# Norm products of local queries and keys: from VectorE to GpSimd, with a re-sorted order of units

## Chip, cores and metric

The kernel runs on one core of one Trainium2 chip. The metric is the device time of one execution in microseconds; the median of three runs is compared. A profiled execution gives the trace.

## What is computed

The input is `x` (4 batches, 512 tokens, 128 features) with a small context of 77 tokens per batch. Each batch goes through three parts:

- **A:** a cross attention of 16 heads to the context, then a layer norm;
- **two local layers**, each a local attention of 8 heads of 64 with windows of 64 tokens, and a gated feed-forward part;
- **C:** a second cross attention with a bias on its scores, then a feed-forward part with activations rounded to 8-bit integers.

The change lies in the local attention. Its queries and keys are normalised per head and turned by a rotary table:

```
q, k = l2norm(q) * q_scale, l2norm(k) * k_scale      # per head of 64
q = q * cos * scale + rotate_half(q) * sin * scale
k = k * cos / scale + rotate_half(k) * sin / scale
sim = einsum(q * 8, k) in windows of 64 and the 64 tokens before
out = softmax(masked sim) @ v;  x = x + out @ wo
```

The inverse norm is a factor per token and head, so the kernel turns first and multiplies by it last.

## The kernel before

Tokens lie on the 128 partitions; a batch is 4 tiles of 128 tokens. All work is cut into units (some instructions of one engine), in streams: X and V (cross attention: scores, values), Z (feed-forward of C, and the norm that ends A), P (projection, rotary and norm of local queries and keys), T (local scores), U (local output), F (local feed-forward). P, T, U and F each have 8 items, one for each batch and layer, in the order of `BLOCKS`. The text numbers them 0 to 7. Each engine plays its units in a fixed order, written in the table `ORDER` ("P3 U1" is three P units, then one U unit). An engine's instructions run strictly in that order, and every one waits by semaphores for what it needs. So a unit that waits holds up all units behind it on its engine.

One item of P goes like this. TensorE turns the input (L761) and projects it in 8 products `QK` (L768), a tile's queries and keys apart. ScalarE squares each bank (L957). VectorE multiplies the bank by cosine into `rot_a` (L1273) and by sine into `rot_b` (L1274), and sums the squares of each tile (L1277). GpSimd adds `rot_b` to `rot_a` (L589, one instruction of 128x1024 for each tile). When all four tiles are summed, VectorE works out 64 inverse norms for each token by Newton steps (L1025 to L1031, into `inv_norm`), and then multiplies each tile of `rot_a` by them in place (L1286, 128x1024, four instructions for each item, each in a unit of its own). Each signals `qk_ready`, on which TensorE waits before it transposes that tile (L780, called QKT here), the first step of T. The next item's cosine products into the same tile of `rot_a` wait for that transposition.

Others that matter: L1258 on VectorE copies half of the next item's projection input out of PSUM (`hT_l`), before which TensorE can't begin that item's L768. L596 on GpSimd multiplies the local probabilities by the inverse row sums that VectorE makes in L1302, and TensorE transposes them in L812. L1294 is VectorE's maximum of local scores, L1322 the gate of F, L1221 the hidden layer of C, L1332 the sum that ends a batch's local layers. L605, L610 and L557 are small GpSimd instructions of F and of the norms.

Of the kernel before, what the change touches and what calls it, by code (L numbers as in the profile page):

```python
# [154 lines left out]
def bank_order():  # L155
# [9 lines left out]
    for group in cross_groups():  # L165
# [11 lines left out]
        "Z2 U32 Z6",  # L177
    "gpsimd":
# [3 lines left out]
    "tensor":  # L182
# [14 lines left out]
    "scalar":  # L197
# [11 lines left out]
    "vector":  # L209
# [11 lines left out]
}  # L221


# [1165 lines left out]
```

## Time and profile before

| | |
|---|---|
| median of 3 runs | 790.55 us (790.01 to 792.83) |
| the profiled execution | 790.43 us |
| its span, first to last instruction | 788.5 us |
| TensorE busy | 618.3 us, 78% |
| VectorE busy | 579.0 us, 73% |
| ScalarE busy | 434.2 us, 55% |
| GpSimd busy | 198.7 us, 25% |

The busy shares are means over stages: a start in which batches' A parts run, a long middle in which the eight local items run, and an end with the C parts. The profiled execution lies 0.12 us under the median of the runs.

### The profile page before, as it was taken

The page shows a single profiled execution, that of the slowest core. Times are in us where ns is not written, and L with a number is a line of the kernel's source. Part 1 is how long each engine was busy: PE and PEld are TensorE (multiplying, and loading weights), DVE is VectorE, ACT ScalarE, POOL GpSimd, SP SyncE. Part 2 cuts the span into 40 slices and gives each one's busy share as a digit, 9 for nine tenths or more (in the row PEclk, how much of TensorE's full clock was granted, in tenths as well). Part 3 has the DMA queues.
Part 4 walks back from the last instruction along what each step waited for, and adds up shares of the span by engine and source line. Part 5 has one row for each costly group of instructions (what it writes and reads, how often), then busy time and mean ns, then how long its engine had stood idle before and what let it go on. Part 6 is the DMA issues. An engine that isn't in the chain of part 4 may idle for free.

```text
span 788.5 us, 15899 instructions
## 1 busy us (share of the span) xinstructions
PE 618.3 (78%) x6108; PEld 413.3 (52%) x6108; DVE 579.0 (73%) x1341; ACT 434.2 (55%) x1076; POOL 198.7 (25%) x133
## 2 busy tenths in 40 slices
PE   5777659879997876877886999678879988887622
PEld 3554434556656653645554565554466675555411
DVE  5659796786877466667658777897577758989965
ACT  2324316754767573586576478456765774632722
POOL 2001241332252144134343122321632121111010
PEclk9789978999999999999999999879989997885865
DMA  7380002001000200010200110002002000000000
GB/s 214 106 168 1 1 0 48 2 2 27 22 2 2 47 2 1 21 28 1 47 2 1 26 23 2 1 1 48 1 2 61 2 1 1 2 14 1 2 13 14
DMA packets 27975, 18.96 MB, mean 24 GB/s; under 512 B 14879, under 2 KB 23677, under 8 KB 27901
## 3 DMA queue, kind: packets, MB, share of 16 engines
q1 hardware_dynamic: 27180, 17.82, 9.5%
q8 instruction: 49, 0.80, 0.4%
q10 hardware_dynamic: 720, 0.13, 0.1%
q14 instruction: 26, 0.21, 0.1%
HBM read 9.56 MB, written 1.05 MB: 13 GB/s over the span
## 4 chain that ended last, share of the span: by engine, by line
PE 43%; DVE 28%; ACT 11%; issue 10%; SPq 4%; POOL 2%; DMA 1%; DVEq 0%; POOLq 0%; ACTq 0%
PE ps L768 6%; PE ps L692 5%; PE ps L856 4%; SPq L529 3%; ACT probs_l L974 3%; PE ps L656 3%; PE ps L793 3%; PE ps L833 3%; PE ps L805 3%; PE ps L812 2%; PE ps L780 2%; DVE rot_b L1274 2%; PE ps L863 2%; PE ps L680 2%; DVE probs L1145 2%
## 5 line engine op out<-in xcount | busy, mean ns | idle before, releaser
L596 POOL TENSOR_TENSOR probs_l<-probs_l,row_sum_l 128x1024 f32<-128x1024 f32 x32 | 63.4, 1981 | 223.5 <-DVE row_sum_l L1302 223.5
L974 ACT ACTIVATE probs_l<-ps,neg_max_l 128x128 f32<-128x128 f32 x256 | 90.6, 379 | 16.2 <-DVE neg_max_l L1294 16.0
L589 POOL TENSOR_TENSOR rot_a<-rot_a,rot_b 128x1024 f32<-128x1024 f32 x32 | 75.1, 2355 | 59.0 <-DVE rot_b L1274 59.0
L768 PE MATMUL ps<-wqkv,hT_l 128*128 128x512 f32 x128 | 72.1, 646 | 19.9 <-DVE rot_b L1274 16.2
L1273 DVE TENSOR_TENSOR rot_a<-ps,rot 128x512 f32<-128x512 f32 x64 | 43.9, 687 | 52.1 <-ACT squares L957 42.9
L920 ACT ACTIVATE probsT<-ps 128x512 f32<-128x512 f32 (+1 forms) x96 | 47.2, 527 | 45.2 <-PE ps L680 45.0
L656 PE MATMUL ps<-k_diag,hT 32*128 32x308 f32 x256 | 63.1, 533 | 10.1 <-DVE probs L1150 3.6
L856 PE MATMUL ps<-hT_f,w 128*128 128x512 f32 x96 | 52.9, 633 | 16.3 <-ACT gelu_g L1007 7.3
L957 ACT ACTIVATE squares<-ps 128x512 f32<-128x512 f32 x64 | 38.7, 605 | 48.1 <-PE ps L768 40.4
L680 PE MATMUL ps<-ident,probs 128*128 128x128 f32 x320 | 53.4, 301 | 6.0 <-ACT probs L909 1.9
L974 ACT ACTIVATION_READ_ACCUMULATOR probs_l<-ps,neg_max_l 128x1 f32 x256 | 56.0, 219 | 0.0
L909 ACT ACTIVATE probs<-probs 128x1232 f32<-128x1232 f32 x32 | 39.7, 1239 | 27.8 <-DVE probs L1150 16.8
L680 PEld LDWEIGHTS ps<-ident,probs 128*128 128x128 f32 x320 | 39.1, 153 | 26.9 <-issue 15.1
L823 PE MATMUL ps<-probsT_l,v_win 128*64 128x64 f32 x1024 | 38.5, 230 | 15.8 <-ACT probsT_l L988 15.6
L1294 DVE TENSOR_REDUCE neg_max_l<-ps 128x4 f32<-128x512 f32 x64 | 42.6, 683 | 10.8 <-PE ps L793 10.5
L988 ACT ACTIVATE probsT_l<-ps 128x512 f32<-128x512 f32 x64 | 35.3, 602 | 27.5 <-PE ps L812 27.3
L823 PEld LDWEIGHTS ps<-probsT_l,v_win 128*64 128x64 f32 x1024 | 34.3, 143 | 29.1 <-ACT probsT_l L988 19.6
L780 PE MATMUL ps<-ident,rot_a 128*128 128x128 f32 x256 | 39.1, 294 | 12.0 <-issue 5.6
L692 PE MATMUL ps<-probsT,v_flat 128*32 128x128 f32 x832 | 40.2, 307 | 10.4 <-ACT probsT L920 6.8
L692 PE MATMUL ps<-probsT,flat_ones 128*32 128x128 f32 x832 | 46.8, 300 | 0.0
L557 POOL TENSOR_TENSOR root_Z<-spread_Z,minus_half 128x4 f32<-128x4 f32 x16 | 16.2, 1012 | 120.6 <-DVE spread_Z L1041 73.8
L656 PEld LDWEIGHTS ps<-k_diag,hT 32*128 32x128 f32 x256 | 26.5, 206 | 36.1 <-issue 10.1
(165 smaller groups left out, 1374.4 us busy)
## 6 DMA issues: line engine op xcount, KB each, us to landing
v_win<-v_win SPq DMA_DIRECT2D x56, 128.0 KB, 2.3
score_bias<-fside_1x16xSxS SPq DMA_DIRECT2D x4, 616.0 KB, 8.7
wqkv<-L_ffn_wqkv SPq DMA_DIRECT2D x2, 768.0 KB
x_res<-x SPq DMA_DIRECT2D x4, 256.0 KB
out<-x_res SPq DMA_DIRECT2D x4, 256.0 KB, 2.3
w<-L_ffn_w SPq DMA_DIRECT2D x6, 128.0 KB
rot_a<-L_ffn_w SPq DMA_DIRECT2D x2, 256.0 KB, 4.2
probs_l<-c_rot SPq DMA_DIRECT2D x1, 512.0 KB
```

The costliest lines, as they stand in the source:

```text
L589: g.tensor_tensor(rot_a[:, t], rot_a[:, t], rot_b[:, t % 2], ALU.add).then_inc(rot_added.sem, 1)
L596: g.tensor_tensor(w, w, row_sum_l[:, t].unsqueeze(2).to_broadcast([P, LH, P]), ALU.mult).then_inc(probs_ready.sem, 1)
L656: mm(to[:, 0:GK].rearrange("p (h k) -> p h k", h=GH), hT[rows, tile(t)], k_diag[rows], start=True, stop=True, tile_position=(32 * grp, 0)) ...
L680: last = tr(to[:, tile(c - a)], probs[:, t % 2, tile(c)], ident)
L692: last = mm(to[32 * grp:32 * grp + 32, tile(part)], of[:, i], probsT[:, tile(c)], start=first, stop=final, tile_position=(0, 32 * grp), sk ...
L768: mm(to, hl[:, tile(t)], wqkv[:, l, k * INNER:(k + 1) * INNER], start=True, stop=True).then_inc(ps.fill(it, "QK", t, k), 1)
L780: last = tr(to[:, tile(c)], rot_a[:, t, tile(k * CH + c)], ident)
L823: last = mm(to[heads, c * P + j * WIN:c * P + (j + 1) * WIN], v_win[:, 2 * t + j, at:at + LD], probsT_l[:, half, c * P + j * WIN:c * P + ( ...
L856: mm(to, w1[:, l, (1 - k) * HC + c], hT_f, start=True, stop=True).then_inc(ps.fill(it, "F", c, k), 1)
L920: a(probsT[:, first * P:end * P], ps.bank(it, "PT", t, n)[:, 0:(end - first) * P], ACT.Copy).then_inc(ps.empty(it, "PT", t, n), 1)
L974: last = a(probs_l[:, t % 2, tile(hd)], ps.bank(it, "S", t, half)[:, tile(c)], ACT.Exp, bias=neg_max_l[:, t, hd:hd + 1], accum_out=row_sum ...
L1273: v.tensor_tensor(rot_a[:, t, cols].rearrange("p (h d) -> p h d", h=LH), x3, cos, ALU.mult)
```

## The change

The four products of each item move from VectorE's P stream to the end of GpSimd's P stream, behind its four additions. A new semaphore `norm_ready` tells GpSimd that the inverse norms are there. Since `inv_norm` is now read by GpSimd, VectorE's Newton steps of an item wait for the products of the item before. VectorE's P stream falls from 144 to 112 units, GpSimd's rises from 32 to 64; the other streams keep their units on each engine. All five rows of `ORDER` are new.

```diff
 ORDER = {
     "sync":
-        "Z2 U32 Z6",
+        "Z4 U26 Z1 U6 Z3",
...
@@ gpsimd, proj_units
                     g.tensor_tensor(rot_a[:, t], rot_a[:, t], rot_b[:, t % 2], ALU.add).then_inc(rot_added.sem, 1)
                     yield
+                pool.wait_ge(*norm_ready(it))
+                for t in tiles:
+                    pool.wait_ge(*rot_added(it, t))
+                    qk = rot_a[:, t].rearrange("p (h d) -> p h d", d=LD)
+                    g.tensor_tensor(qk, qk, inv_norm[:, t * 2 * LH:(t + 1) * 2 * LH].unsqueeze(2).to_broadcast([P, 2 * LH, LD]),
+                                    ALU.mult).then_inc(qk_ready.sem, 1)
+                    yield
@@ vector, proj_units
                 dve.wait_ge(*squares_used(it, TILES - 1))
+                if it.index:
+                    dve.wait_ge(*qk_ready(before(it), TILES - 1))
                 rsqrt(inv_norm, *(newton[:, i] for i in range(3)), ALU.max, 1e-24)
-                yield
-                for t in tiles:
-                    dve.wait_ge(*rot_added(it, t))
-                    qk = rot_a[:, t].rearrange("p (h d) -> p h d", d=LD)
-                    v.tensor_tensor(qk, qk, inv_norm[:, t * 2 * LH:(t + 1) * 2 * LH].unsqueeze(2).to_broadcast([P, 2 * LH, LD]),
-                                    ALU.mult).then_inc(qk_ready.sem, 1)
-                    yield
+                dve.sem_inc(norm_ready.sem, 1)
+                yield
```

In the new kernel the lines of GpSimd's products and additions are L595 and L589, of the probabilities L603; everything further down is 7 lines lower.

VectorE at the end of item 3's norms, before: the last Newton step, the four products, then item 4's copy of `hT_l` and its first rotary products.

```order
L1029 TENSOR_TENSOR newton<-newton 128x64
L1030 SCALAR_TENSOR_TENSOR newton<-newton 128x64
L1031 SCALAR_TENSOR_TENSOR inv_norm<-newton 128x64
L1286 TENSOR_TENSOR rot_a<-rot_a,inv_norm 128x1024 x4
L1257 MEMSET hT_l 64x1
L1258 COPY hT_l<-ps 64x511
L1273 TENSOR_TENSOR rot_a<-ps,rot 128x512
L1274 TENSOR_TENSOR rot_b<-ps,rot 128x512
```

The same place in the changed kernel:

```order
L1036 TENSOR_TENSOR newton<-newton 128x64
L1037 SCALAR_TENSOR_TENSOR newton<-newton 128x64
L1038 SCALAR_TENSOR_TENSOR inv_norm<-newton 128x64
L1264 MEMSET hT_l 64x1
L1265 COPY hT_l<-ps 64x511
L1280 TENSOR_TENSOR rot_a<-ps,rot 128x512
L1281 TENSOR_TENSOR rot_b<-ps,rot 128x512
```

The products are gone and the copy follows the Newton steps at once. The same holds for item 0; at items 4 to 6 a unit or two stand between.

GpSimd from item 3's last three additions on, before: the probabilities of item 3, then F and item 4's first addition.

```order
L589 TENSOR_TENSOR rot_a<-rot_a,rot_b 128x1024 x3
L596 TENSOR_TENSOR probs_l<-probs_l,row_sum_l 128x1024
L605 TENSOR_TENSOR h_l<-y_res,one 128x4x64
L589 TENSOR_TENSOR rot_a<-rot_a,rot_b 128x1024
L557 TENSOR_TENSOR root_F<-spread_F,minus_half 128x4
```

The same place in the changed kernel:

```order
L589 TENSOR_TENSOR rot_a<-rot_a,rot_b 128x1024 x3
L595 TENSOR_TENSOR rot_a<-rot_a,inv_norm 128x1024 x2
L617 TENSOR_TENSOR y_res<-y_res,b_row 128x512
L595 TENSOR_TENSOR rot_a<-rot_a,inv_norm 128x1024 x2
L589 TENSOR_TENSOR rot_a<-rot_a,rot_b 128x1024
L603 TENSOR_TENSOR probs_l<-probs_l,row_sum_l 128x1024
```

The first product stands right behind the additions; a small addition of F has moved between the products, and item 4's first addition ahead of the probabilities.

TensorE ahead of item 2's first transposition of `rot_a`, before: its last projection, then value units of the cross attention.

```order
L768 MATMUL ps<-wqkv,hT_l 128x512
L680 MATMUL ps<-ident,probs 128x128 x8
L629 MATMUL ps<-ident,ctx_in 128x77
L680 MATMUL ps<-ident,probs 128x128 x2
L692 MATMUL ps<-probsT,v_flat 32x128 x13
L692 MATMUL ps<-probsT,flat_ones 32x128 x13
L823 MATMUL ps<-probsT_l,v_win 64x64 x16
L780 MATMUL ps<-ident,rot_a 128x128 x8
```

The same place in the changed kernel, from ten rows ahead of the transposition:

```order
L863 MATMUL ps<-hT_f,w 128x512
L687 MATMUL ps<-ident,probs 128x128 x2
L699 MATMUL ps<-probsT,v_flat 32x128 x13
L699 MATMUL ps<-probsT,flat_ones 32x128 x13
L636 MATMUL ps<-ident,ctx_in 128x77
L687 MATMUL ps<-ident,probs 128x128 x8
L863 MATMUL ps<-hT_f,w 128x512
L687 MATMUL ps<-ident,probs 128x128 x2
L699 MATMUL ps<-probsT,v_flat 32x128 x13
L699 MATMUL ps<-probsT,flat_ones 32x128 x13
L863 MATMUL ps<-hT_f,w 128x512
L787 MATMUL ps<-ident,rot_a 128x128 x8
```

More units stand between the item's last projection and its first transposition here: 12 now, 6 before. At the other items the number changes by three at most (3 to 4, 8 to 11, 2 to 3, 5 to 6, 8 to 10, 7 to 9, 6 to 5).

## Rows read from the trace of the kernel before

**Rows 1.** Busy time by stage, all engines (windows)

```profile
core 0: us, PE busy (x) PEld busy (x) DVE busy (x) ACT busy (x) POOL busy (x), PEclk, DMA share, GB/s
...
114.00:595.00 481.00, 399.28 (x3964) 264.71 (x3965) 339.75 (x719) 303.38 (x828) 149.26 (x86) 0.94 0.07 15
595.00:788.00 193.00, 141.19 (x1435) 96.09 (x1433) 155.59 (x390) 97.91 (x195) 28.39 (x23) 0.79 0.05 11
```

**Rows 2.** The page: the chain that ended last, by engine

```profile
PE 43%; DVE 28%; ACT 11%; issue 10%; SPq 4%; POOL 2%; DMA 1%; DVEq 0%; POOLq 0%; ACTq 0%
```

**Rows 3.** L1286 alone by stage; then durations and who waited

```profile
114.00:595.00 481.00, 40.47 (x32) 0.94 0.07 15
```

**Rows 4.** L1286, L596 and L1274: durations min/median/max ns (source view)

```profile
L1286 DVE TENSOR_TENSOR rot_a<-rot_a,inv_norm x32: 1172/1217/2918, 114.3 to 594.5; 128x1024 f32<-128x1024 f32 x32
L596 POOL TENSOR_TENSOR probs_l<-probs_l,row_sum_l x32: 1894/1896/2876, 134.5 to 646.0; 128x1024 f32<-128x1024 f32 x32
L1274 DVE TENSOR_TENSOR rot_b<-ps,rot x64: 674/680/682, 73.5 to 571.2; 128x512 f32<-128x512 f32 x64
```

**Rows 5.** Groups by line and form: busy us, mean ns, idle before

```profile
L589 POOL TENSOR_TENSOR rot_a<-rot_a,rot_b 128x1024 f32<-128x1024 f32 x32 | 75.1, 2355 | 59.0 <-DVE rot_b L1274 59.0
L1025 DVE TENSOR_SCALAR newton<-newton 128x64 f32<-128x64 f32 x8 | 5.2, 654 | 0.1
```

**Rows 6.** The chain in order of time, places with L1286 (start, us)

```profile
316.53 2.87 DVE rot_a L1286 x3
...
319.94 1.22 DVE rot_a L1286
...
321.29 0.70 DVE hT_l L1258
...
425.86 4.61 DVE rot_a L1286 x4
...
518.44 1.21 DVE rot_a L1286
...
529.35 2.27 DVE rot_a L1286 x2
```

**Rows 7.** Timeline at items 0 and 6: product, then TensorE's transposition

```profile
114.32 4.63 DVE L1286 TENSOR_TENSOR rot_a<-rot_a,inv_norm 128x1024 f32<-128x1024 f32 x4
...
115.64 1.94 PE L780 MATMUL ps<-ident,rot_a 128*128 128x128 f32 x8 [5.63 <-issue]
...
518.44 1.21 DVE L1286 TENSOR_TENSOR rot_a<-rot_a,inv_norm 128x1024 f32<-128x1024 f32 x1
...
519.71 1.97 PE L780 MATMUL ps<-ident,rot_a 128*128 128x128 f32 x8 [0.52 <-DVE rot_a L1286]
519.84 1.90 POOL L596 TENSOR_TENSOR probs_l<-probs_l,row_sum_l 128x1024 f32<-128x1024 f32 x1 [4.95 <-DVE row_sum_l L1302]
```

**Rows 8.** Timeline at item 1: VectorE and GpSimd side by side

```profile
168.06 2.36 POOL L589 TENSOR_TENSOR rot_a<-rot_a,rot_b 128x1024 f32<-128x1024 f32 x1 [4.44 <-DVE rot_b L1274]
...
169.07 1.40 DVE L1025 TENSOR_SCALAR newton<-newton 128x64 f32<-128x64 f32 x1
...
175.75 4.01 DVE L1286 TENSOR_TENSOR rot_a<-rot_a,inv_norm 128x1024 f32<-128x1024 f32 x2
...
175.91 2.77 POOL L596 TENSOR_TENSOR probs_l<-probs_l,row_sum_l 128x1024 f32<-128x1024 f32 x1 [5.49 <-DVE row_sum_l L1302]
```

**Rows 9.** TensorE at item 5, timeline around the four products

```profile
427.86 2.94 PE L863 MATMUL ps<-w,gated 128*128 128x128 f32 x24
430.64 1.04 PE L780 MATMUL ps<-ident,rot_a 128*128 128x128 f32 x8
431.52 1.02 PE L768 MATMUL ps<-wqkv,hT_l 128*128 128x512 f32 x2
```

**Rows 10.** Waits from 114 to 595 us (total, times, longest)

```profile
DVE rot_a L1273 <- ACT squares L957: 40.6, 31, 2.7
...
PE ps L768 <- DVE rot_b L1274: 13.1, 16, 2.3
```

More of the change, by code:

```diff
@@ L436, in build @@
         rot_added = counter("rot_added", proj, tiles)
+        norm_ready = counter("norm_ready", proj)
         qk_ready = counter("qk_ready", proj, tiles)
```

77 rows, old and new, of the table ORDER are left out of this document.

## Prediction

> **What bounds the kernel now.** I read the windows first, then the chain, then single places of the timeline. All 32 products lie in the stage from 114 to 595 us (but for the last one's end). There TensorE is busy 399.3 of 481 us (83%), VectorE 339.8 (71%), ScalarE 303.4 (63%) and GpSimd 149.3 (31%), at a granted clock of 0.94 [rows 1]. Nobody is full: the eight local items are a relay, and time goes where one engine hands over to the next. The stage from 595 us on is another matter, VectorE has 155.6 of 193 us, but the change takes next to nothing from it. Over the whole span TensorE makes up 43% of the chain and VectorE 28% [rows 2]. So VectorE is the second owner of the path and GpSimd (2%) has room. That speaks for the move but doesn't price it, for VectorE waits a lot as well: 40.6 us ahead of L1273 for ScalarE's squares alone [rows 10].
>
> Which products are on the path? The chain in order of time passes through L1286 at three items only: 2.87 and 1.22 us at item 3, 4.61 at item 5, 1.21 and 2.27 at item 6, together 12.2 of the 40.5 us [rows 3, 6]. At item 3 it goes on into L1258: the copy that opens item 4's projection started at 321.29, behind all four products, where the inverse norms were there at 316.5. There the change removes real path, and the order rows of VectorE show that the copy now follows the Newton steps at once.
>
> The second thing that I looked for is who waits for the first product. At item 0 the first of the four products starts at 114.32 and TensorE's transposition at 115.64, after 5.63 us of idleness. At item 6 the product runs from 518.44 to 519.65 and the transposition starts at 519.71 [rows 7]. I looked at all eight items: in six (0, 1, 2, 3, 4 and 6) TensorE starts within 0.1 us of the first product's end; at items 5 and 7 it comes 3.6 and 3.7 us later. The other three products of an item are 12 us or more early everywhere. So the first product is a hand-over on TensorE's path and the other three only cost VectorE's time.
>
> **The change, part by part.** All terms are against the profiled execution, 790.43 us, 0.12 under the median of 790.55.
>
> 1. *Products off VectorE's chain.* Removed: 12.2 us of chain [rows 6]. Not all of it is gained. At item 5 TensorE is busy with L863 from 427.86, QKT from 430.64, and L768, which needs the copy, starts at 431.52, right as QKT's issue ends [rows 9]. With the copy 4.6 us earlier TensorE doesn't come earlier; only VectorE's own backlog behind it shrinks. I give up rather more than half of those 4.6, 2.6 us. Term: -12.2 + 2.6 = -9.6.
>
> 2. *The first product on GpSimd.* The trace has no such instruction on GpSimd. The nearest is L596: one 128x1024 operand times a broadcast one, median 1896 ns. The farther one is L589, two full operands, 2355 ns [rows 4, 5]. On VectorE the product has a median of 1217 ns. The new one is L596's form with another broadcast (64 instead of 128 elements long), so I take 1.90 and keep 2.36 as the upper bound. Nothing below VectorE's 1.22 is plausible, as both GpSimd rows are far above it. A hand-over VectorE to GpSimd is quick: at item 6 GpSimd's L596 starts at 519.84, 0.13 us after TensorE got the first product, with the reciprocal that released it in between [rows 7]; I add 0.07 for it. Term: six items x (1.90 - 1.22 + 0.07) = +4.5. At 2.36 it would be six x 1.21 = +7.3. At items 5 and 7 the 3.6 us of slack cover it; without that cover it would be 1.5 more.
>
> The Trainium skill (GPSIMD Engine Reference, Performance versus the Vector engine) speaks against the move: elementwise work with two inputs belongs on VectorE, GpSimd measured 1.96 times slower in a large addition. By that ratio the product would take an estimated 2.4 us, the term would be about +7 and the forecast some 2.6 us later. This trace agrees for two full operands (2355 against 1217) and not for a broadcast one (1896 is 1.56 times).
>
> 3. *The other three products.* They run one behind another, 1.9 us each, so the fourth is ready about 7.6 us after the norms where it was ready after 4.6. They are needed 12 us later at the earliest, so: nothing. What hides them is the distance between two transpositions of an item; it would be gone only if a long unit stood between them on GpSimd's queue. GpSimd goes from 149.3 to 149.3 + 32 x 1.9 = 210 us, 44% of the stage.
>
> 4. *What is behind them on GpSimd.* The order rows of item 3: its products now stand ahead of item 4's first addition and of item 3's probabilities (now L603), and one small addition of F is between them. Behind the products TensorE waits for the probabilities (L812). At item 0 the first product starts at 114.3 and the first probabilities at 134.5 [rows 4], so 7.6 us of products are hidden there. Nothing in this term, but it is where a stall would go next.
>
> 5. *The two engines in each other's way.* At item 1 L1025, a tiny Newton instruction, took 1.40 us: it started at 169.07 while GpSimd's addition ran from 168.06 to 170.42, and ended with it. The mean of the eight is 654 ns. Then two products took 4.01 us in place of 2.4, and GpSimd's L596 beside them 2.77 in place of 1.90 [rows 4, 5, 8]; that pair happened twice, at items 1 and 4, the second on the chain. With the products gone from VectorE these two pairs vanish: -0.9 on the path. In return GpSimd is busy 60.8 us more, 13% of the stage, in which a Newton instruction can meet it. Eight Newton starts now lose (654 - 180) x 8 = 3.8 us in all, 180 being what L1025 takes undisturbed; with 41% more GpSimd time that grows by 1.5, of which I put 1.0 on the path. Term: -0.9 + 1.0 = +0.1.
>
> 6. *The new order.* TensorE's order barely changes. Item 2 has 12 units between last projection and first transposition where it had 6, which covers the slower product; at the others it moves by three at most. All that moves is the same work, so its price is that of the waits it makes or removes, and I have no row for them: 0, with -5 and +5 as bounds, five being about the largest single wait of TensorE in this stage (5.63, item 0) [rows 7]. SyncE's queue now stores the first finished batch before the last six of the V moves. In the trace that batch is done before the first of these moves is due, so nothing waits. The extra wait of the Newton steps for the products of the item before is met some 40 us early.
>
> 7. *VectorE's relief where it isn't on the chain.* TensorE's 13.1 us of waits for L1274 in the stage [rows 10] could shrink with a VectorE 12% less loaded (40.5 of 339.8). I count 12% of it, 1.6, against the part of term 1 that another chain may take, and leave both out.
>
> Sum: -9.6 + 4.5 + 0.1 = -5.0, that is 785.4 us.
>
> **Rivals.**
> - *A, slower: the first product comes late from GpSimd's queue.* It now stands behind the additions and sometimes behind probabilities (item 1: behind those of item 0's last tile). If in each of the eight items it starts one instruction of 1.9 us late and takes 1.9, TensorE waits 8 x (0.68 + 1.9) = 20.6 us more, against 12.2 removed: 798.8. It decides from an average delay of about 1.5 us an item on. Against it: the additions end before the norms do (item 1: the last addition ends at 170.42, the second product began at 175.75 [rows 8]) and GpSimd idles 69% of the stage. Chance 0.14.
> - *B, slower or even: blocking.* If every VectorE instruction that can be held up like L1025 meets GpSimd in the added 13% and waits half of 1.9 us, with some 100 such groups in the stage, that is 12 us of VectorE's time, on the path by between a quarter and all of it: 788.4 to 797, midpoint about 792. For it: L1025's 1.40 us [rows 8]. Against: most of VectorE's work here read PSUM and one SBUF operand, and L1274, of that kind, has the same duration at all 64 places, GpSimd busy or idle [rows 4]. The Trainium skill (SBUF — State Buffer, Who interferes with whom) has this as a rule: instructions of VectorE with two SBUF inputs or in a 2-port mode and those of GpSimd shut each other out for their whole length. By that rule the trace agrees at items 1 and 4, and the change also removes 32 such instructions. Chance 0.10.
> - *C, no change: the removed work was not the bound.* Other chains of ScalarE and TensorE lie just under this one, they take all but 4 or 5 us of the 12.2, and the first product gives that back: 788 to 792. For it: VectorE's 40.6 us of waits for the squares. Chance 0.20.
> - *D, a larger gain.* The whole 12.2 counts, half of the 13.1 us of waits for L1274 goes too, and the new order hides the slower first product (item 2's does): 790.4 - 12.2 - 0.9 - 6.5 + 1.5 = 772.3, say 774. Chance 0.10.
>
> **From these to the numbers.** The forecast has 0.46, with a range of its own from 780 to 789: down to 780 if the new order saves 5, up by 2.8 for the 2.36 us product. Under 774 D and over 797 A leave out a tenth each, so the range is 774 to 797. A measurement of this kernel tells a change of 0.5%, 4 us, from none. Faster by that (under 786.6): four fifths of the forecast's 0.46, D, and a little of C: 0.50. Slower (over 794.5): A, a third of B, and the tail of a bad order, 0.03: 0.20. The same: the rest, 0.30.
>
> **What would show it.** Right: GpSimd's products at 1.9 us, VectorE's busy time down by about 41 us and GpSimd's up by 61, `hT_l`'s copy directly behind the Newton steps, TensorE's first transposition waiting for GpSimd by up to 2 us at most items, the stage from 114 us to the end of item 7 shorter by about 5, and the last stage unchanged. Wrong: products of 2.4 us or more; a wait of 3 us or more for the product at several items (A); L1025 or other small VectorE instructions of over 1 us at more than three items (B); VectorE's idle time up by all of the 40 us (C).

## The result: slower by 0.6%, and the profile after

The changed kernel has a median of 796.17 us in 11 runs (794.57 to 798.27), the kernel before 792.83 us in 11 runs beside it (789.07 to 798.39). The ratio is 1.0058, with a 95% interval from 1.0030 to 1.0086. Executions that ran in a slower state are left out of the ratios here and below, one of 3056 us in the first experiment among them. The two medians lie 3.3 us apart, and the ratio says 4.6 us (2.4 to 6.8), to the wrong side of no change; the forecast was 5 us to the other. The profiled execution took 795.31 us, its span is 793.2.

The page of the changed kernel, its line of busy time and its chain by engine (the latter answers to [rows 2]):

```profile
PE 616.3 (78%) x6108; PEld 412.3 (52%) x6108; DVE 544.5 (69%) x1309; ACT 441.6 (56%) x1082; POOL 255.8 (32%) x165
...
PE 48%; DVE 21%; ACT 17%; issue 8%; SPq 4%; POOL 1%; DMA 1%; DVEq 0%; POOLq 0%; ACTq 0%
```

VectorE's share of the chain fell from 28 to 21%, and the time did not fall with it: TensorE and ScalarE took it over. The windows by stage, columns as in [rows 1]:

```profile
114.00:595.00 481.00, 396.32 (x3978) 261.67 (x3979) 306.89 (x697) 309.11 (x836) 207.07 (x119) 0.95 0.07 16
595.00:793.20 198.20, 137.72 (x1418) 95.48 (x1416) 152.87 (x376) 98.28 (x192) 26.89 (x22) 0.79 0.03 7
```

VectorE lost 32.9 us in the local stage and GpSimd took on 57.8, over the whole span 34.5 and 57.1, where the forecast had 41 and 61. VectorE's idle time over the span rose from 209.5 to 248.7 us, by 39.2: more than all of its relief. The product and the probabilities on GpSimd, in the source view (L603 answers to L596 of [rows 4]), with the waits for the first of them:

```profile
L595 POOL TENSOR_TENSOR rot_a<-rot_a,inv_norm x32: 1891/1902/2348, 113.2 to 591.9; 128x1024 f32<-128x1024 f32 x32
its engine sat idle before it (us, times) until:
  DVEq L1291: 21.8, 7
who waited for it (us, times):
  PEld ps L787: 1.6, 3
...
L603 POOL TENSOR_TENSOR probs_l<-probs_l,row_sum_l x32: 1887/1896/1897, 127.5 to 642.1; 128x1024 f32<-128x1024 f32 x32
```

The product takes 1.90 us, and in the whole kernel TensorE waits 1.6 us for it. Waits of the local stage that answer to [rows 10]:

```profile
DVE rot_a L1280 <- ACT squares L964: 50.2, 35, 3.3
...
PE ps L775 <- DVE rot_b L1281: 9.1, 11, 2.0
```

VectorE's wait for the squares grew from 40.6 to 50.2 us: some 10 of its 33 us of relief became idle time at this one place. In time the changed kernel is ahead for long. Item 7's first transposition, in the timeline of the kernel before and then of the changed one:

```profile
583.70 1.04 PE L780 MATMUL ps<-ident,rot_a 128*128 128x128 f32 x8
```

```profile
575.69 1.41 PE L787 MATMUL ps<-ident,rot_a 128*128 128x128 f32 x8
```

It comes 8 us earlier, but most of that is the order itself, which has it sooner: at items 3, 4 and 6 the first transposition is 2.1 to 2.5 us ahead, at item 5 by 0.8. The end of the span comes 4.7 us later. So the change does two things of opposite sign, one before this point and one after it, and the experiments begin by taking them apart.

### The profile page after: what moved, and what is told of

Same layout as the page of the kernel before. It is cut to its first block, busy times and chain, and to the rows that moved or that the text cites. A ratio compares the mean times of both kernels' runs of the same rounds, so it can differ in the third digit from the quotient of the medians.

```text
span 793.2 us, 15920 instructions
## 1 busy us (share of the span) xinstructions
PE 616.3 (78%) x6108; PEld 412.3 (52%) x6108; DVE 544.5 (69%) x1309; ACT 441.6 (56%) x1082; POOL 255.8 (32%) x165
## 4 chain that ended last, share of the span: by engine, by line
PE 48%; DVE 21%; ACT 17%; issue 8%; SPq 4%; POOL 1%; DMA 1%; DVEq 0%; POOLq 0%; ACTq 0%
PE ps L699 7%; PE ps L775 6%; PE ps L663 4%; ACT probs_l L981 4%; PE ps L800 4%; PE ps L863 4%; SPq L529 3%; PE ps L840 3%; PE ps L812 3%; PE ps L687 3%; ACT squares L964 2%; PE ps L830 2%; PE ps L787 2%; PE ps L795 2%; PE ps L819 2%
## 5 line engine op out<-in xcount | busy, mean ns | idle before, releaser
L603 POOL TENSOR_TENSOR probs_l<-probs_l,row_sum_l 128x1024 f32<-128x1024 f32 x32 | 60.7, 1896 | 167.5 <-DVE row_sum_l L1306 167.5
L589 POOL TENSOR_TENSOR rot_a<-rot_a,rot_b 128x1024 f32<-128x1024 f32 x32 | 75.3, 2358 | 72.7 <-DVE rot_b L1281 72.7
L663 PE MATMUL ps<-k_diag,hT 32*128 32x308 f32 x256 | 65.8, 563 | 17.9 <-DVE probs L1157 6.5
L595 POOL TENSOR_TENSOR rot_a<-rot_a,inv_norm 128x1024 f32<-128x1024 f32 x32 | 60.7, 1915 | 21.8 <-DVEq L1291 21.8
L964 ACT ACTIVATE squares<-ps 128x512 f32<-128x512 f32 x64 | 38.7, 605 | 50.2 <-PE ps L775 49.3
L995 ACT ACTIVATE probsT_l<-ps 128x512 f32<-128x512 f32 x64 | 35.1, 603 | 27.1 <-PE ps L819 26.8
L1193 DVE RECIPROCAL inv_sum<-ps 128x128 f32<-128x128 f32 x32 | 30.5, 954 | 23.3 <-PE ps L699 22.9
L699 PEld LDWEIGHTS ps<-probsT,v_flat 128*32 128x32 f32 x832 | 30.2, 121 | 30.3 <-issue 20.8
```

What stands on the lines that cost most here:

```text
L589: g.tensor_tensor(rot_a[:, t], rot_a[:, t], rot_b[:, t % 2], ALU.add).then_inc(rot_added.sem, 1)
L595: g.tensor_tensor(qk, qk, inv_norm[:, t * 2 * LH:(t + 1) * 2 * LH].unsqueeze(2).to_broadcast([P, 2 * LH, LD]), ALU.mult).then_inc(qk_ready ...
L603: g.tensor_tensor(w, w, row_sum_l[:, t].unsqueeze(2).to_broadcast([P, LH, P]), ALU.mult).then_inc(probs_ready.sem, 1)
L663: mm(to[:, 0:GK].rearrange("p (h k) -> p h k", h=GH), hT[rows, tile(t)], k_diag[rows], start=True, stop=True, tile_position=(32 * grp, 0)) ...
L699: last = mm(to[32 * grp:32 * grp + 32, tile(part)], of[:, i], probsT[:, tile(c)], start=first, stop=final, tile_position=(0, 32 * grp), sk ...
L964: a(squares[:, k], ps.bank(it, "QK", t, k), ACT.Square).then_inc(ps.empty(it, "QK", t, k), 1)
```

## The experiments

Ratios are to the kernel before on the same chip, with 95% intervals; 1% is 7.9 us. "Head" is each engine's order of units until item 7's first transposition, "tail" what is left then. A kernel with another head or tail takes the same units in another row of its order table and is the same elsewhere.

**1. The move and the order apart.** Three kernels have the products on GpSimd, one keeps them on VectorE. With the old head, GpSimd's products stand where VectorE began them in the trace before.

```diff
 # GpSimd's row, its end: changed kernel (-), new head with old tail (+)
-"P3 F1 P1 U1 P3 U1 X1 F1 P2 F1 U2 F1 U2 X1 Z2 F1 Z1 F2 Z1 X1 Z8"
+"P3 F1 P1 U1 P5 U1 X1 F1 U1 F1 U1 F1 U1 X1 U1 Z2 F3 Z2 X1 Z8"
```

Old head, old tail:

> The products move to GpSimd, but all five rows of the order stay as before: VectorE only loses its product units, and GpSimd's are inserted at the places in time where VectorE began them. Theory 1 (the move gains a little, the new order of the end loses it): 785 to 789 against 790.5, ratio 0.994 to 0.998, and the start of item 7's first transposition some 3 us earlier than before. Rival (the move itself costs: a slower first product and more GpSimd work): ratio 1.003 or more, with TensorE waiting for the product at most items.

Measured: 1.0175 (1.0148 to 1.0202).

New head, old tail:

> The changed kernel with the new order until item 7's first transposition (cut at one unit count on each engine), then what is left in the order of before. Theory 1: the 5 us of lead that the changed kernel has at item 7's V products stays until the end: 785 to 788, ratio 0.993 to 0.997. Rival (the move costs in the end too, or the end is lost whatever its order): 794 to 797, ratio 1.005 as the changed kernel.

Measured: 0.9972 (0.9948 to 0.9996).

Old head, new tail:

> The products on GpSimd, the order of before until item 7's first transposition, then the new order. Theory 1: the end costs 9 to 10 us over the first run of this set, ratio 1.005 to 1.012. Rival: equal to the first run of this set within 0.3%.

Measured: 1.0252 (1.0219 to 1.0285).

New head, new tail, products on VectorE:

> The new order on all engines, the products kept on VectorE, as many units behind the Newton steps as before. Theory 1: as the new end costs 10 us and the products stay on VectorE, slower than the changed kernel: 798 to 804, ratio 1.010 to 1.017. Rival (the move costs, the order is neutral): within 0.3% of before.

Measured: 1.0353 (1.0333 to 1.0373). The move alone costs 1.75%, the order alone 3.5%, and both together 0.6%. With the products moved, the new head gives 2.0 to 1.9% back (1.0175 to 0.9972, 1.0252 to 1.0058), and the new tail costs 0.8 to 0.9%. The price of the move can't be told without the order around it. Three of the four lie outside all that I had expected, on the slow side; new head with old tail came as forecast.

**2. Is the hand-over the cost?** Three kernels: products of an item's second to fourth tile as late as possible on GpSimd, behind the probabilities that are due; then, in two orders, the first product back on VectorE. And the kernel before with no product at all.

```diff
 # first product back on VectorE, behind the Newton steps
+dve.wait_ge(*rot_added(it, TILES - 1))
+qk = rot_a[:, 0].rearrange("p (h d) -> p h d", d=LD)
+v.tensor_tensor(qk, qk, inv_norm[:, 0:2 * LH]..., ALU.mult).then_inc(qk_ready.sem, 1)
 # kernel before without products
-v.tensor_tensor(qk, qk, inv_norm[...]..., ALU.mult).then_inc(qk_ready.sem, 1)
+dve.sem_inc(qk_ready.sem, 1)
```

> All five rows as in the run with the move under the old order (ratio 1.0175), but on GpSimd's row the products of tiles 1 to 3 stand as late as their transpositions and the next item's additions allow, behind the probabilities that are due before. Theory 1 (products ahead of probabilities on GpSimd's queue hold up TensorE's L812 transpositions): ratio falls to 1.003 to 1.010. Rival (the slower first product, six hand-overs of 0.7 us and what hangs on them, or blocking of small VectorE instructions): within 0.3% of 1.0175.

Measured: 1.0140 (1.0083 to 1.0196). Theory 1 missed: TensorE's waits for the probabilities fell from 7.3 to 0.4 us, and the ratio by 0.0035, with an interval of 0.0062 to both sides, so no gain is shown.

> Old order, products of tiles 1 to 3 on GpSimd as late as in the run beside it, the product of tile 0 stays on VectorE where it was (it waits for all four additions). Theory 1 (queue position): equal to the run beside it within 0.4%. Rival (the first product's hand-over is the cost): 0.5 to 1% below the run beside it, 0.993 to 1.000 of before.

Measured: 1.0148 (1.0103 to 1.0194).

> New order until item 7's first transposition, old order behind it (0.9972 of before with all products on GpSimd), tile 0's product on VectorE directly behind the Newton steps (one unit later at item 1). If the first product's hand-over costs 0.7 us at six items also in the new order: 0.991 to 0.994. If the new order hides it: 0.996 to 0.999.

Measured: 1.0073 (1.0042 to 1.0104), where all four on GpSimd gave 0.9972: outside both expectations.

> The kernel before without the 32 products (queries and keys stay unnormalised; everything else and the order are as before): the ceiling of what relieving VectorE can give in the old order. If the 12.2 us of the chain are path, as the prediction counted: 0.984 to 0.988. If other chains lie just under it: 0.993 to 0.998.

Measured: 0.9926 (0.9884 to 0.9969). With the first product on VectorE the old order shows no saving (1.0148 against 1.0140, but the difference is only known to 0.7%, 6 us, either way), and the new head is 1% slower. So the hand-over is not the cost in the new head, and not shown to be one in the old order. And what taking the products off VectorE can give in the old order is 5.9 us (2.4 to 9.2), less than the 9.6 of the sum's first term.

**3. GpSimd's load by itself, and the products' price in the new order.** The first two kernels let GpSimd do work that nobody waits for, at the places of the products:

```diff
+pool.wait_ge(*norm_ready(it))
+for t in tiles:
...
+    for i in range(4):
+        n = 16 * it.index + 4 * t + i
+        if n:
+            pool.wait_ge(spare_used.sem, n)
+        g.tensor_tensor(pair(spare), pair(row2[:, 0:248]), row2[:, 0:8].unsqueeze(2).to_broadcast([P, 8, 31]), ALU.mult).then_inc(spare_used.sem, 1)
+    yield
```

> Order of before, and no product on VectorE at all; GpSimd does the same amount of work as in the kernel with moved products, at the same 32 places of its queue (each product as four multiplications of 248 columns of a constant row into a spare tile, released by the norms), but TensorE does not wait for them: it takes the unnormalised queries and keys when their additions and norms are there. This leaves the normalisation out. Without any product the ratio was 0.993, with the products moved under this order 1.018. If GpSimd's load is what the move costs (its queue, and VectorE held up beside it), the ratio is 1.008 to 1.018. If it is TensorE's waiting for the product, it is 0.990 to 0.998. In between, both.

Measured: 1.0319 (1.0274 to 1.0364).

> The kernel before, whole, with its products on VectorE, and in addition GpSimd's spare multiplications at the same 32 places as in the run above. Nothing waits for them but GpSimd's own queue. If GpSimd's load costs by itself: 1.010 to 1.025, since here VectorE's products can also meet them (a pair of the two took 4.0 in place of 2.4 us in the profile before). If the load costs nothing: 1.000 to 1.005.

Measured: 1.0725 (1.0681 to 1.0770). Both are outside every expectation, so their waits come first. TensorE's largest group of waits in each (total, times, longest), first in the run with the products left out, then in the one that keeps VectorE's products:

```profile
PE ps L825 <- POOL probs_l L609: 23.9, 7, 7.0
```

```profile
PE ps L825 <- POOL probs_l L609: 37.1, 7, 8.6
```

The spare work in the groups of these two, in the same order:

```profile
L602 POOL TENSOR_TENSOR spare<-b_row 128x248 f32<-128x248 f32 x128 | 78.1, 610 | 35.7 <-DVEq L1296 26.7
```

```profile
L602 POOL TENSOR_TENSOR spare<-b_row 128x248 f32<-128x248 f32 x128 | 100.8, 788 | 35.9 <-DVEq L1296 26.9
```

In the kernel before, this wait is 2.0 us. The local probabilities go through GpSimd, and where they stand behind four blocks of spare work of 2.4 us and more each, TensorE stands too. The spare work is longer than real products (four pieces of 610 ns where VectorE has none, of 788 where it has its own, against 1902), so the two runs overstate the load. What they show is where such a load bites in the old order. TensorE's waits for the probabilities grow by 21.9 and 35.1 us, of a loss of 25 and 57; its waits for VectorE's products are 5.9 us in the second run against 3.1 before. That real products bite there too is not shown by them, and the run with late products speaks against it.

> The fastest version so far (products on GpSimd, new order until item 7's first transposition and old order behind it, ratio 0.997) without its products: GpSimd hands the tiles on when norms and additions are there. This leaves the normalisation out. If the new order hides the moved products fully, the ratio stays 0.995 to 0.998. If the products still hold TensorE up by some 0.75 us or more at each of eight items, it falls to 0.985 to 0.992. If the old order's loss of 14 us from the move came from waiting and the new order only hides that, this is close to the 0.993 that the old order had without products.

Measured: 0.9905 (0.9872 to 0.9938).

> Products on VectorE, new order until item 7's first transposition, old order behind it. With the new order everywhere and the products on VectorE the ratio was 1.035; the new order's last stage cost 0.008 twice. If the two add up, this is 1.024 to 1.030: the new order of the local stage is only good for the moved products. If the loss of that run sat in the last stage, it is 0.995 to 1.005, and the order of the local stage would be the gain by itself.

Measured: 1.0200 (1.0164 to 1.0236), between the two expectations. Why the new head is so bad with products on VectorE, its waits say, and then its timeline at item 3:

```profile
PE ps L767 <- DVE hT_l L1257: 20.1, 5, 7.2
```

```profile
326.18 0.23 DVE L1030 SCALAR_TENSOR_TENSOR inv_norm<-newton 128x64 f32<-128x64 f32 x1
326.44 4.63 DVE L1285 TENSOR_TENSOR rot_a<-rot_a,inv_norm 128x1024 f32<-128x1024 f32 x4
...
331.20 0.69 DVE L1257 COPY hT_l<-ps 64x511 f32<-64x511 f32 x1
...
332.04 2.05 PE L767 MATMUL ps<-wqkv,hT_l 128*128 128x512 f32 x2 [7.20 <-DVE hT_l L1257]
```

The same place with the products on GpSimd (new head, old tail):

```profile
311.00 0.23 DVE L1038 SCALAR_TENSOR_TENSOR inv_norm<-newton 128x64 f32<-128x64 f32 x1
...
311.54 0.69 DVE L1265 COPY hT_l<-ps 64x511 f32<-64x511 f32 x1
...
312.38 1.10 PE L775 MATMUL ps<-wqkv,hT_l 128*128 128x512 f32 x2 [1.26 <-DVE hT_l L1265]
```

And in the kernel before, where TensorE does item 3's transposition and four more groups first:

```profile
317.81 1.09 PE L780 MATMUL ps<-ident,rot_a 128*128 128x128 f32 x8 [0.76 <-DVE rot_a L1286]
318.74 0.60 PE L761 MATMUL ps<-ident,y_res 128*128 128x128 f32 x4
...
320.67 1.10 PE L793 MATMUL ps<-kT_l,qT_l 64*64 64x128 f32 x32
322.13 1.10 PE L768 MATMUL ps<-wqkv,hT_l 128*128 128x512 f32 x2 [0.35 <-DVE hT_l L1258]
```

The new head asks for the copy `hT_l` as soon as the norms are done and the old one only when the products are. So each order hides the products in one place alone. A table of all ratios, measured on three chips, each beside the kernel before:

| head / tail | no products | on VectorE | on GpSimd |
|---|---|---|---|
| old / old | 0.9926 | 1 | 1.0175 |
| new / old | 0.9905 | 1.0200 | 0.9972 |
| new / new | 1.0020 | 1.0353 | 1.0058 |
| old / new | | | 1.0252 |

In the old order the products cost 5.9 us on VectorE and 19.7 on GpSimd; in the new head 23.4 on VectorE and 5.3 on GpSimd. Without products the two heads differ by 0.2%, which the intervals don't tell from none. (There VectorE hands the tiles on in the old order, GpSimd in the new one.)

**4. Where the tail loses.** The changed kernel's order until a given time, and the old order for what had not begun by then.

> The changed kernel's order until what it began by 605 us, the order of before for all that was left then. Changed over at item 7's first transposition (575 us) the ratio was 0.997, never changed over 1.006. In the profile of the changed kernel item 7's products are 5 us ahead of the kernel before at 590 to 600 us and the lead is lost between 605 and 640. If the loss is made by the order of 605 to 640: 0.995 to 0.999. If it is the order of 575 to 605 (item 7's last two products behind the probabilities and F's first addition): 1.003 to 1.007.

Measured: 0.9953 (0.9923 to 0.9982).

> The same, changed over at 646 us. By then the changed kernel's lead of 5 us is gone in its profile and 4.7 us more are lost between 660 and 710. If all of the loss is made before 646: 1.003 to 1.007, if half of it: 0.999 to 1.003, if none: 0.995 to 0.999.

Measured: 0.9971 (0.9942 to 0.9999).

> The changed kernel's order until what it began by 690 us, the order of before for what is left. Changed over at 646 us the ratio was 0.997, never changed over 1.006. If the loss is made in the order of 646 to 690 us: 1.003 to 1.007. If it is made behind 690: 0.996 to 1.000. In between: both.

Measured: 0.9983 (0.9957 to 1.0010).

> The changed kernel without its products (this leaves the normalisation out); its GpSimd hands the tiles on when norms and additions are there. With the order of before behind item 7's first transposition the ratio was 0.9905. If the last part's new order costs 0.8% whatever becomes of the products: 0.997 to 1.001. If its price hangs on the products: 0.989 to 0.994.

Measured: 1.0020 (0.9985 to 1.0055). My reading of the profile, a lead lost between 605 and 640 us, was wrong: with the new order kept until 646 nothing is lost. Most of the 0.8% is made behind 690 us, long after the last product, and it is there without products too (0.9905 to 1.0020). Windows behind 646 us, columns time, busy TensorE, its granted clock, DMA; the changed kernel, then the one that changes over at 646:

```profile
646.00:700.00 54.00, 44.29 (x442) 0.84 0.01 1
700.00:800.00 100.00, 48.66 (x440) 0.70 0.03 9
```

```profile
646.00:700.00 54.00, 46.29 (x474) 0.91 0.01 1
700.00:800.00 100.00, 41.68 (x411) 0.72 0.03 9
```

In the first window TensorE's granted clock is 0.84 against 0.91 and it gets through 32 instructions fewer; 7 us more of its busy time are left behind 700. This is one execution of each. Which exchange in the cross stage's orders makes the difference is not settled; VectorE's, ScalarE's and TensorE's orders there differ together.

**5. GpSimd's queue, with the real products.** One row of the kernel with new head and old tail:

```diff
-"P3 F1 P1 U1 P5 U1 X1 F1 U1 F1 U1 F1 U1 X1 U1 Z2 F3 Z2 X1 Z8"
+"P3 F1 P1 U1 P3 U1 X1 P2 F1 U1 F1 U1 F1 U1 X1 U1 Z2 F3 Z2 X1 Z8"
```

> The version with ratio 0.997, with item 6's last probabilities and the small root instruction ahead of item 7's third and fourth product on GpSimd instead of behind them. Its profile had TensorE wait 4.0 us for these probabilities, which GpSimd began at 577.95 us, behind 7.93 us of products. If that wait is on the path: 0.991 to 0.995 (up to 4 us less). If another chain lies just under it: 0.996 to 0.999.

Measured: 0.9925 (0.9894 to 0.9955), 786.64 us, the lowest ratio of all versions that compute everything. The timeline with all four products ahead of the probabilities, and with two of them behind:

```profile
570.06 7.93 POOL L595 TENSOR_TENSOR rot_a<-rot_a,inv_norm 128x1024 f32<-128x1024 f32 x4 [3.78 <-DVEq L1291]
577.95 1.89 POOL L603 TENSOR_TENSOR probs_l<-probs_l,row_sum_l 128x1024 f32<-128x1024 f32 x1
...
579.89 1.97 PE L819 MATMUL ps<-ident,probs_l 128*128 128x128 f32 x8 [4.04 <-POOL probs_l L603]
```

```profile
571.93 4.21 POOL L595 TENSOR_TENSOR rot_a<-rot_a,inv_norm 128x1024 f32<-128x1024 f32 x2 [3.77 <-DVEq L1291]
576.90 1.90 POOL L603 TENSOR_TENSOR probs_l<-probs_l,row_sum_l 128x1024 f32<-128x1024 f32 x1 [0.77 <-DVE row_sum_l L1306]
...
578.86 1.97 PE L819 MATMUL ps<-ident,probs_l 128*128 128x128 f32 x8 [0.68 <-POOL probs_l L603]
```

The wait went from 4.04 to 0.68 us, and the ratio fell by 0.0047, which is 3.7 us (0.6 to 6.8; the two kernels ran on different chips, each beside the kernel before). That the wait alone is worth this is not shown: the kernel that changes over at 605 us has two products behind these probabilities as well, TensorE waits 1.6 us for probabilities in all of it, and its ratio is 0.9953.

The last run went after the old order's loss. In the kernel with late products, item 3 has this timeline:

```profile
397.72 3.76 POOL L596 TENSOR_TENSOR rot_a<-rot_a,inv_norm 128x1024 f32<-128x1024 f32 x2
...
400.06 1.45 DVE L1049 TENSOR_SCALAR spread_F<-mv_F 128x4 f32<-128x4 f32 x1
...
401.44 2.36 POOL L590 TENSOR_TENSOR rot_a<-rot_a,rot_b 128x1024 f32<-128x1024 f32 x1
...
403.76 1.02 POOL L558 TENSOR_TENSOR root_F<-spread_F,minus_half 128x4 f32<-128x4 f32 x1
404.82 0.35 DVE L1055 TENSOR_SCALAR h_l<-h_l,mv_F,root_F 128x128 f32<-128x128 f32 x1 [1.52 <-POOL root_F L558]
...
407.09 0.60 ACT L965 ACTIVATE squares<-ps 128x512 f32<-128x512 f32 x1 [2.19 <-DVE newton L1285]
...
409.16 1.22 PE L776 MATMUL ps<-wqkv,hT_l 128*128 128x512 f32 x1 [4.41 <-DVE rot_b L1282]
```

A VectorE instruction of 0.17 us takes 1.45 and ends with GpSimd's product; the small root stands behind an addition; and four engines pass the delay on.

```diff
 # GpSimd's units at this place
-P3 F2
+P2 F1 P1 F1
```

> The kernel with the order of before and the products as late as possible on GpSimd (ratio 1.014), with one exchange in GpSimd's order: item 3's F root (128x4, 1.02 us), which stood behind two products and an addition and began 2.2 us late, now goes ahead of that addition. In the profile of the run with 1.014 VectorE then waited 1.5 us for it, ScalarE 2.2 us for VectorE, and TensorE's lag grew by 2.1 us there. If that place is worth what the lag says: 1.010 to 1.0125. If the relay takes it up: 1.013 to 1.016.

Measured: 1.0164 (1.0130 to 1.0198). Nothing gained. The exchange put another delay in the place of the one that it took: the root is done sooner, but the four `h_l` instructions of VectorE behind it now run beside GpSimd's addition and take 2.56 us, where they took 1.11.

Where the old order loses can be seen in the traces. In the three kernels with the old head and all or most products on GpSimd (at VectorE's places; late; all but the first), item 3's first transposition starts 2.5 to 4.1 us later than in the kernel before, item 4's 6.2 to 6.9, item 5's 11.6 to 12.9, and item 7's 11.4 to 13.1. So most of it is made between items 3 and 5. Windows from item 3's first transposition to item 5's, columns as in [rows 1]: the kernel before, the products at VectorE's places, all but the first on GpSimd.

```profile
317.80:430.60 112.80, 91.22 (x868) 59.35 (x869) 74.39 (x139) 76.77 (x214) 38.44 (x21) 0.98 0.08 18
```

```profile
321.30:443.50 122.20, 99.03 (x868) 64.18 (x869) 60.55 (x130) 76.97 (x214) 59.01 (x33) 0.92 0.07 16
```

```profile
320.30:442.30 122.00, 98.63 (x869) 63.79 (x870) 64.36 (x132) 77.02 (x214) 50.58 (x28) 0.92 0.07 16
```

The stretch is 9.4 and 9.2 us longer, and 7.8 and 7.4 us of that is TensorE busy for longer with the same products, at a granted clock of 0.92 where the kernel before has 0.98. TensorE's waits add only 1 to 2 us. With late products it is 5.1 of 7.9 us, at 0.93. These are single executions, and what makes the clock fall there is not shown.

## Why the prediction was wrong, step by step

1. **Products off VectorE's chain (-9.6).** This step failed. I took the share of the chain that runs through L1286 [rows 3, 6] for time that can be won. Without any product the old order wins 5.9 us (2.4 to 9.2). The trace had the row against it: TensorE waits 0.35 us for item 4's copy at item 3, since its own order puts other work ahead. The chain says who was last, not by how much.
2. **The first product on GpSimd (+4.5).** The duration was right (1.90 us expected, 1.902 measured). The term was over-sized: TensorE waited 3.1 us in all for VectorE's product before, and waits 1.6 us for GpSimd's in the changed kernel, 4.3 in the old order, where the term charged six full delays. (The other sum beside it, with 2.4 us for a product, comes to +7.5 and 3.0 us, not +7 and 2.6.)
3. **The other three products (0).** TensorE doesn't wait for these tiles; in the changed kernel they are 3.9 us early or more. Right.
4. **What is behind them on GpSimd (0).** Right for the changed kernel: its own order keeps the waits for probabilities at 1.6 us in two places. But I named the place "where a stall would go next" and priced it from item 0 alone, where the probabilities come 20 us later. In the old order with real products TensorE waits 7.3 us for them where it waited 2.0, though taking that wait away brought no clear gain; at item 7 of the new head with the old tail there is one wait of 4.0 us, and splitting the block there gave 3.7 us (0.6 to 6.8).
5. **The two engines in each other's way (+0.1).** About right. Time that VectorE's instructions took over the median of their form, summed from the trace: 12.0 us before, 12.4 after. So rival B did not decide here. It is not nothing elsewhere: in the two old-order kernels with late products the same sum is 16.0.
6. **The new order (0, bounds 5).** This is the step that failed and decided. With the products moved, the head's new order is worth -16 us and the tail's +6.8 (give or take 2.9), and this +6.8 is what turned the sign. I bounded both by TensorE's largest single wait [rows 7]. An order has hundreds of places, and a single wait bounds none of their sum. "TensorE's order barely changes" was a misreading: I had looked only between an item's last projection and its first transposition, while 422 of TensorE's 603 units stand at another place of its row, 56 of them by more than three.

The sum of a term per edit assumed that the edits add. They don't: the move from VectorE to GpSimd is +13.9 us in the old order and -18.1 with the new head. In its own terms the change is sound (old order and VectorE 1, new head and GpSimd 0.9972), gains 2.2 us, and loses 6.8 in the cross stage's new order, which the move does not need. None of the rivals was this; C, the removed work was not the bound, comes nearest, and its sign, VectorE's idle time up by 40 us, came out (39.2).

What stays open: which exchange behind 690 us costs the 0.8%, and why the old order loses 14 us. TensorE's waits for GpSimd don't explain it, though they grow by 6.5 (7.3 and 4.3, from 2.0 and the 3.1 for VectorE's product): with late products and the first one on VectorE they are 0.4 us, and the ratio is still 1.0148. The traces have 5 to 8 us of it as TensorE busy for longer at a lower granted clock between items 3 and 5, without a cause for the clock.

## What to carry to other kernels

A chain shows which work was last at each step; what removing it is worth has to be read from the waits of the engine that needs it, at that place, in that order. Where an order of units was fitted to where the work runs, work and order are one edit, and the price of either alone says nothing about both: measure the cells of the table. When work goes to a queue, ask for every other client of that queue how long it may stand behind the new block, and split the block where the answer is short.

## What I had not expected of the hardware

**The granted clock varies from execution to execution of one kernel, and the time with it.** In 103 executions of the kernel before, made beside the experiments, the span's granted clock goes from 0.885 to 0.907 and the time from 785 to 800 us; a straight line through them has 5.2 us for 0.01 of clock (correlation -0.86). The line does not carry over to another kernel: of the changed one, three executions at 0.910 have a mean of 795.2 us and seven at 0.897 one of 796.8, 1.6 us for 0.013. Which of the two drives the other is not shown. The kernel with new head and old tail was profiled at 783.66 us and 0.912, its median is 791.33 with 0.899. So a single profile can be off by more than this change is worth. The medians of the clock are 0.897 after and 0.898 before, so it tells nothing of the 0.6%; the old order with moved products has 0.891 against 0.900 of the kernel before beside it, which goes with the longer busy time seen above.

**ScalarE's functions alternate more in the new order.** Groups of the changed kernel, then of the kernel before:

```profile
L1014 ACT ACT_TABLE_LOAD x19 | 24.4, 1283 | 0.3
...
L916 ACT ACT_TABLE_LOAD x6 | 7.7, 1283 | 0.1
```

```profile
L1007 ACT ACT_TABLE_LOAD x16 | 20.5, 1283 | 0.3
...
L909 ACT ACT_TABLE_LOAD x5 | 6.4, 1283 | 0.1
```

In all 46 loads against 40, at 1.283 us each, 7.7 us more of ScalarE. Some of them are on the chain that ended last. One each from the kernel before and the changed one, in the chain in order of time:

```profile
347.13 1.28 ACT L1007
```

```profile
687.40 1.28 ACT L1014
```

There are eleven such pieces in either chain, 14.1 us. So the six more loads take no more of the chain than before; whether they cost anything was not shown.
